# The second expert stage on token rows sorted by expert, instead of every expert on every token

## The reference

```
logits = xt @ router_w.T                      # 2048 tokens, 8 experts
topk_vals, topk_idx = top_k(logits, 2)
g = sigmoid(topk_vals); g = g / (g.sum(-1) + 1e-10)
for e in range(8):
    ge = sum(where(topk_idx == e, g, 0))      # 0 where e is not among the token's two
    h = silu(xt @ w_gate[e]) * (xt @ w_up[e]) # 128 -> 256
    out += ge * (h @ w_down[e])               # 256 -> 128
```

## Time and profile before

| | |
|---|---|
| median of three runs | 820.43 us |
| the profiled execution | 818.59 us |
| its span, first to last instruction | 816.6 us |
| granted clock of PE, mean | 0.996 |
| PE busy | 778.5 us, 95% |
| DVE busy | 627.8 us, 77% |
| ACT busy | 525.5 us, 64% |
| POOL busy | 420.0 us, 51% |

### The profile page before, as it was taken

The page is one execution under the profiler, slowest core; times in us unless marked ns, Lnnn a source line. Parts: engine busy times, 40 slices in busy tenths (PEclk is TensorE's granted clock), DMA queues, the critical chain, the costliest instruction groups (busy, mean ns, idle before and its releaser), DMA issues.

```text
span 816.6 us, 13532 instructions
## 1 busy us (share of the span) xinstructions
PE 778.5 (95%) x4328; PEld 544.7 (67%) x4328; DVE 627.8 (77%) x1600; ACT 525.5 (64%) x1163; POOL 420.0 (51%) x443
## 2 busy tenths in 40 slices
PE   4988899999889999999999999999999999999998
PEld 2666688886556666675666666766656667778886
DVE  7988688789799757779767778667696957877787
ACT  6556566655677767666767757667567755556654
POOL 1053999984334333333433334334335435699973
PEclk9999999999999999999999999999999999999999
DMA  8012454481000000000000000000010061254201
GB/s 231 3 43 27 107 128 97 67 302 77 1 2 1 1 1 2 1 2 1 2 1 1 2 1 1 1 2 0 2 40 14 27 91 44 54 113 92 77 13 53
DMA packets 51157, 35.16 MB, mean 43 GB/s; under 512 B 2656, under 2 KB 48608, under 8 KB 51088
## 3 DMA queue, kind: packets, MB, share of 16 engines
q1 hardware_dynamic: 51088, 34.30, 17.3%
HBM read 33.04 MB, written 1.25 MB: 42 GB/s over the span
## 4 chain that ended last, share of the span: by engine, by line
PE 77%; DVE 11%; ACT 4%; issue 4%; DMA 2%; POOL 2%; SPq 0%; DVEq 0%; POOLq 0%; ACTq 0%
PE psum L1004 14%; PE psum L986 12%; PE psum L971 11%; PE psum L249 10%; PE psum L524 8%; PE psum L250 8%; PE psum L251 8%; PE psum L928 4%; DVE prob L1104 2%; POOL hid_lo L816 2%; ACT x_norm L315 1%; DMA gate_all<-gates 1%; DVE hid L678 1%; DVE hid L658 1%; DVE ln_stats L264 1%
## 5 line engine op out<-in xcount | busy, mean ns | idle before, releaser
L1369 POOL TENSOR_SCALAR prob<-prob,ones 128x512 f32<-128x512 f32 x256 | 173.9, 692 | 272.2 <-DVE ones L1093 272.2
L1272 ACT ACTIVATE prob<-prob,ones 128x512 f32<-128x512 f32 x256 | 183.6, 719 | 124.4 <-DVE ones L1104 124.4
L816 POOL TENSOR_TENSOR hid_lo<-hid,hid_hi 128x512 fp32r<-128x512 f32 x125 | 187.1, 1512 | 73.6 <-ACT hid_hi L598 72.1
L1104 DVE CUSTOM_DVE_ANT_0 prob<-psum,bias_band 128x512 f32<-128x512 f32 x256 | 161.6, 687 | 71.3 <-PE psum L971 70.5
L678 DVE TENSOR_TENSOR hid<-hid,gate_all 128x512 f32<-128x512 f32 x118 | 117.6, 999 | 14.8 <-DMA gate_all<-gates 3.7
L1004 PE MATMUL psum<-probT,v 128*64 128x512 f32 x512 | 124.0, 605 | 0.0
L986 PE MATMUL psum<-ident,prob 128*128 128x128 f32 x1024 | 123.3, 273 | 0.0
L986 PEld LDWEIGHTS psum<-ident,prob 128*128 128x128 f32 x1024 | 114.6, 140 | 10.3 <-issue 2.8
L658 DVE TENSOR_TENSOR hid<-silu,psum 128x512 f32<-128x512 f32 x128 | 87.2, 683 | 43.6 <-PE psum L251 33.9
L591 ACT ACTIVATE silu<-psum 128x512 f32<-128x512 f32 x128 | 76.2, 597 | 65.4 <-PE psum L251 64.8
L598 ACT CAST hid_hi<-hid 128x512 fp32r<-128x512 f32 x128 | 78.5, 618 | 55.7 <-DVE hid L678 52.1
(11 more groups left out here) (165 smaller groups left out, 1204.3 us busy)
## 6 DMA issues: line engine op xcount, KB each, us to landing
gate_all<-gates SPq DMA_DIRECT2D x59, 256.0 KB, 5.4
bias_band<-bias_rows SPq DMA_DIRECT2D x16, 448.0 KB, 9.2
w_raw<-in_w_gate SPq DMA_DIRECT2D x16, 128.0 KB, 2.8
w_raw<-in_w_up SPq DMA_DIRECT2D x16, 128.0 KB, 2.8
w_raw<-in_w_down SPq DMA_DIRECT2D x16, 128.0 KB, 3.5
x_res<-in_x SPq DMA_DIRECT2D x4, 256.0 KB, 6.0
out<-x_res SPq DMA_DIRECT2D x3, 256.0 KB, 2.3
wqT<-in_WqT SPq DMA_DIRECT2D x1, 512.0 KB, 7.6
```

Source lines behind the costliest of these rows:

```text
L816: nc.gpsimd.tensor_tensor(m["hid_lo"][:, s % 2, half, :], m["hid"][:, s % DEEP, half, :], m["hid_hi"][:, s % 2, half, :].bitcast(F32), ALU ...
L1104: nc.vector.tensor_tensor_reduce(out=prob[:, buf, h, :], in0=bank[scores_home(n) + h][:, :], in1=row_bias, scale=-1.0, scalar=NEG_START, o ...
L1272: nc.scalar.activation(prob[:, buf, h, :], prob[:, buf, h, :], ACT.Exp, bias=peak[:, buf, h:h + 1], scale=-1.0, accum_out=total[:, buf, h: ...
L1369: nc.gpsimd.tensor_scalar(prob[:, buf, h, :], prob[:, buf, h, :], inv[:, buf, h:h + 1], 1.0, ALU.mult, ALU.mult).then_inc(a_n, 1)
```

## The change

The second expert stage no longer goes over all tokens for each expert. The tokens fall in three groups (chunks 0 and 1, chunk 2, chunk 3). For each group DVE finds the two experts of each token, and counts, with PE's help (`group_count`: a running sum over tiles on DVE, one over partitions by a matmul with a triangle of ones), for each choice its position among its expert's rows. Each expert gets whole blocks of 128 slots. That gives a slot number for each choice of each token, and an expert number for each block. POOL scatters the normalized rows of `x_norm` to their slots in memory (`xs`), one DMA by index for each tile and choice, 32 in all; SP loads them back with the slots on partitions. The numbers of blocks are fixed at their largest values, 23, 15 and 15; slots that nobody takes hold zeros, which SP writes beforehand.

A block on PE: a transpose of its rows (four blocks at a time, `sorted_turn`; ACT and DVE make the high and low halves), the expert's number read from memory into a register, three matmuls with the rows as the stationary side and the 512 gate and up columns of that expert moving, at the address that the register gives (`block_gate_up`), silu on ACT, product on DVE, two transposes (`block_turn`), a copy on ACT, and two full f32 matmuls with `w_down` of that expert (`block_down`). The results of four blocks leave PSUM at a time and are stored to memory (`ys`). POOL gathers them by slot number, 32 DMAs by index, and DVE adds each tile, times its gate, to `x` (`combine`, 32 operations). All eight experts' weights are held and split during the last attention slots (8 casts of 512 columns on ACT, 8 subtractions on POOL, in place of 6 and 6 of 256 columns). The gate broadcasts, the gates in PSUM, the split of the hidden product and the sums over experts in PSUM are gone from this stage. In the fourth batch entry one value projection moves from slots 7, 14, 15 to 14, 15, 18.

The diff, cut; buffers, semaphores, the routing and the calls in the slots are left out.

```diff
-            expert_buffers(1, hid_hi=QK_AT, hid_lo=QK_AT + H * P, hid=IN_BAND(40), silu=WV_AT, y_sum=R(0),
-                           w_hi=[IN_BAND(6), IN_BAND(9), R(68)], w_lo=[IN_BAND(12), IN_BAND(15), R(71)],
-                           w_raw=IN_BAND(0), routing=IN_BAND(18), gate_all=IN_BAND(24)),
...
+        GROUPS = [(0, 2 * QT), (2 * QT, 3 * QT), (3 * QT, 4 * QT)]
+        N_BLOCKS = [(2 * (n1 - n0) * P - E) // P + E for n0, n1 in GROUPS]
+        FIRST_BLOCK = [sum(N_BLOCKS[:g]) for g in range(len(GROUPS))]
+        ALL_BLOCKS = sum(N_BLOCKS)
...
+        QUADS = [(g, b, min(4, nb - b)) for g, nb in enumerate(N_BLOCKS) for b in range(0, nb, 4)]
+        BLOCK = [(q, j) for q, (g, b, n) in enumerate(QUADS) for j in range(n)]
...
+        def group_start(dve, g, home):
+            n, m = tiles_of(g), GRP[g]
+            dve.wait_ge(GS["pm"], g + 1)
+            counts = bank[home][:, 0:E * (n + 1)].rearrange("p (e n) -> p e n", e=E)
+            group_link(dve, nc.vector.tensor_scalar(m["nb"].unsqueeze(2), counts[:, :, n:n + 1], 1.0 / P,
+                                                    (P - 1) / (2.0 * P), ALU.mult, ALU.add))
+            group_link(dve, nc.vector.tensor_scalar(m["nb"], m["nb"], MAGIC, -MAGIC, ALU.add, ALU.add))
+            group_link(dve, nc.vector.tensor_tensor_scan(m["ce"], iota8[:, 1:2].to_broadcast([P, E]), m["nb"], 0.0,
+                                                         ALU.mult, ALU.add))
+            group_link(dve, nc.vector.tensor_tensor(m["st"], m["ce"], m["nb"], ALU.subtract))
+            nc.vector.scalar_tensor_tensor(out=by_expert(g, "pos"), in0=m["st"].unsqueeze(2).to_broadcast([P, E, n]),
+                                           scalar=float(P), in1=counts[:, :, 0:n], op0=ALU.mult,
+                                           op1=ALU.add).then_inc(GS["pb"], 1)
...
+        def group_blocks(dve, g):
...
+            group_link(dve, nc.vector.tensor_tensor(cmp, shared["count"][:, 0:nb].unsqueeze(2).to_broadcast([P, nb, E]),
+                                                    m["ce"].unsqueeze(1).to_broadcast([P, nb, E]), ALU.is_ge))
+            group_link(dve, nc.vector.tensor_reduce(m["bidf"], cmp, mybir.AxisListType.X, ALU.add))
+            nc.vector.tensor_scalar(m["bid"].bitcast(I32), m["bidf"], float(E - 1), None, ALU.min).then_inc(GS["bd"], 1)
...
+        def scatter_rows(pool, g, n, r):
+            pool.wait_ge(GS["sl"], g + 1)
+            pool.wait_ge(GS["zf"], 16 * len(GROUPS))
+            tile = GROUPS[g][0] + n
+            pool.wait_ge(LN[3]["xn"], tile // QT + 1)
+            at = r * tiles_of(g) + n
+            nc.gpsimd.indirect_dma_start(xs_dram[g][:, :], bass.IndirectOffsetOnAxis(
+                GRP[g]["slot"].bitcast(U32)[:, at:at + 1], 0), xn[:, tile, :], None).then_inc(GS["sc"][g], 16)
...
+        def gather_rows(pool, g, n, r):
+            pool.wait_ge(GS["yd"][g], 16 * sum(quad[0] == g for quad in QUADS))
+            tile, at = GROUPS[g][0] + n, r * tiles_of(g) + n
+            landed = GS["gd"][tile // QT] if g < 2 else GS["gt"][n]
+            nc.gpsimd.indirect_dma_start(ys_in[g][:, r, n, :], None, ys_dram[g][:, :], bass.IndirectOffsetOnAxis(
+                GRP[g]["slot"].bitcast(U32)[:, at:at + 1], 0)).then_inc(landed, 16)
...
+        def block_gate_up(pe, i):
+            q, j = BLOCK[i]
+            g, b, n = QUADS[q]
+            pe.wait_ge(GS["xl"], q + 1)
+            if i == FIRST_BLOCK[g]:
+                pe.wait_ge(GS["bd"], g + 1)
+            if i == 0:
+                pe.wait_ge(GS["ws"], E)
+            if i >= 3:
+                pe.wait_ge(GS["mul"], i - 2)
+            expert = pe.value_load(GRP[g]["bid"].bitcast(I32)[0:1, b + j:b + j + 1], min_val=0, max_val=E - 1)
+            expert_of[i] = expert
+            w = bass.ds(expert * (2 * FH), 2 * FH)
+            rows = slice(j * P, (j + 1) * P)
+            three(pe, bank[GATE_BANK + i % 3][:, :], xs_hi[:, q % 2, rows], xs_lo[:, q % 2, rows], ws_hi[:, w],
+                  ws_lo[:, w]).then_inc(GS["gu"], 1)
...
+        def block_turn(pe, i):
+            pe.wait_ge(GS["mul"], i + 1)
+            if i >= 2:
+                pe.wait_ge(GS["hc"], i - 1)
+            for h in range(MT):
+                last = nc.tensor.transpose(bank[HT_BANK + i % 2][:, h * P:(h + 1) * P],
+                                           s_hid[:, i % 3, h * P:(h + 1) * P], ident[:, :])
+            last.then_inc(GS["ht"], 1)
...
+        def block_down(pe, i):
+            q, j = BLOCK[i]
+            pe.wait_ge(GS["hc"], i + 1)
+            if i == 0:
+                pe.wait_ge(GS["wd"], 32)
+            if j == 0 and q > 0:
+                pe.wait_ge(GS["yc"], q)
+            for h in range(MT):
+                last = nc.tensor.matmul(bank[Y_BANK][:, j * P:(j + 1) * P], hT[:, i % 3, h * P:(h + 1) * P],
+                                        ws_down[:, bass.ds(expert_of[i] * (MT * D) + h * D, D)], start=(h == 0),
+                                        stop=(h == MT - 1))
+            last.then_inc(GS["dn"], 1)
...
+        def block_product(dve, i):
+            dve.wait_ge(GS["sg"], i + 1)
+            if i >= 3:
+                dve.wait_ge(GS["ht"], i - 2)
+            nc.vector.tensor_tensor(s_hid[:, i % 3, :], s_silu[:, i % 3, :], bank[GATE_BANK + i % 3][:, FH:2 * FH],
+                                    ALU.mult).then_inc(GS["mul"], 1)
...
+        def quad_out(dve, q):
+            g, b, n = QUADS[q]
+            dve.wait_ge(GS["dn"], QUAD_END[q])
+            nc.vector.tensor_copy(ys_out[g][:, b:b + n, :].rearrange("p b d -> p (b d)"),
+                                  bank[Y_BANK][:, 0:n * P]).then_inc(GS["yc"], 1)
...
+        def combine(dve, g, r, n):
+            tile = GROUPS[g][0] + n
+            c_done[0] += 1
+            gate = by_tile(g, "gw", 2)[:, n, r:r + 1]
+            nc.vector.scalar_tensor_tensor(out=x[:, tile, :], in0=ys_in[g][:, r, n, :], scalar=gate, in1=x[:, tile, :],
+                                           op0=ALU.mult, op1=ALU.add).then_inc(GS["cb"], 1)
...
+                sorted_turn(pe, 0)
                 transposes(SLOTS - 1)
                 pv(SLOTS - PV_LAG + 1)
                 pe.wait_ge(a_m, 2 * SLOTS)
-                part(0, 1)
+                block_gate_up(pe, 0)
                 for n in range(SLOTS - QT, SLOTS):
                     pv(n)
-                part(1, 0)
-                part(1, 1)
-                pe.wait_ge(a_x, part_count(B - 1, 0))
+                block_gate_up(pe, 1)
+                pe.wait_ge(a_ea, SLOTS)
+                pe.wait_ge(a_eb, SLOTS)
+                block_turn(pe, 0)
+                block_gate_up(pe, 2)
+                pe.wait_ge(GS["pb"], 2)
                 for half in range(2):
                     project_out(B - 1, 1, half)
-                part(2, 0)
-                pe.wait_ge(a_ea, SLOTS)
-                down(pe, 1, 0)
-                part(2, 1)
-                part(3, 0)
-                pe.wait_ge(a_eb, SLOTS)
-                down(pe, 1, 1)
-                part(3, 1)
-                part(4, 0)
+                block_turn(pe, 1)
+                sorted_turn(pe, 1)
                 pe.wait_ge(a_o, B * PAIRS)
-                down(pe, 1, 2)
-                part(4, 1)
...
+                block_down(pe, 0)
+                for i in range(3, ALL_BLOCKS):
+                    q, j = BLOCK[i]
+                    block_gate_up(pe, i)
+                    block_turn(pe, i - 1)
+                    block_down(pe, i - 2)
+                    if j == 1 and q + 1 < len(QUADS):
+                        sorted_turn(pe, q + 1)
+                    if i == 7:
+                        ln_turn(pe, 3, 3, JOB_BANK)
+                    if i == 10:
+                        group_logits(pe, 2, JOB_BANK)
+                    if i == 16:
+                        pe.wait_ge(GS["rs"], 3)
+                        group_count(pe, 2, JOB_BANK)
+                block_turn(pe, ALL_BLOCKS - 1)
+                block_down(pe, ALL_BLOCKS - 2)
+                block_down(pe, ALL_BLOCKS - 1)
...
+                sorted_low(dve, 0)
+                for i in range(ALL_BLOCKS):
+                    q, j = BLOCK[i]
+                    block_product(dve, i)
+                    last_chunk(i)
+                    combined(i)
+                    if j == 2 and q + 1 < len(QUADS):
+                        sorted_low(dve, q + 1)
+                    if i >= 2 and BLOCK[i - 2][1] == QUADS[BLOCK[i - 2][0]][2] - 1:
+                        quad_out(dve, BLOCK[i - 2][0])
+                quad_out(dve, len(QUADS) - 1)
+                dve.wait_ge(GS["gd"][2], 16 * 2 * QT)
+                dve.wait_ge(GS["gw"], 3)
+                for r in range(2):
+                    if r == 1:
+                        dve.wait_ge(GS["cb"], c_done[0])
+                    for n in range(QT):
+                        combine(dve, 1, r, n)
+                for n in range(QT):
+                    dve.wait_ge(GS["gt"][n], 32)
```

(32 more changed lines are left out.)

568 lines of the change are left out of this document (353 added, 215 removed).

## The result

| | time, us (median) | span of the profiled run | mean granted clock |
|---|---|---|---|
| before | 818.79 | 816.6 | 0.996 |
| after | 827.95 | 827.7 | 0.958 |

The changed kernel takes 1.0115 times as long, interval 1.0084 to 1.0147: slower by 9 us, where 15 us less were forecast.

The account below looks back on a forecast made before the run. PE, busy 95% of the span, was taken as the bound. The terms 660 + 6 + 10.7 + 102.3 + 5 + 1.5 + 17.6 gave a span of 803 us, and 2 us over the span gave 805; range 783 to 850.

Parts of the forecast that it names:

- In the block stage: Second expert stage: 5 us of PE waiting for DVE's norm and routing, 1.5 filling and draining, later groups' scatters at nothing.
- Pace: Time per block on PE: 1.93 us, from 1.63 for the stream plus 0.3 for DVE's order; 53 blocks 102.3 us.
- 10.7 + 102.3 + 5 + 1.5: Block stage in us: attention work left on PE, 53 blocks, PE waiting for DVE's norm and routing, filling and draining.
- The loaded address: Register load before each block's gate/up matmuls on PE: taken as 0.7 us, between bounds of 0.08 and 1.4.
- Attention: Last quarter of attention: new routing, scatters and POOL's larger subtractions cost 6 us, from 2 to 14; first block about 666.
- The new end: After the last down product: copy, store, eight gathers 1.3 us apart, additions, store; 17.6 us in place of 4.65.
- Rival 1: Register load before each block costs next to nothing: pace 1.65 us, 15 us less, 790 us; chance 0.20.
- Rival 2: Register load before gate/up lies open: 2.55 us a block, 53 blocks 135 us, measured time of 838 us; chance 0.20.
- Rival 3: Index DMAs slow on POOL, 2.5 us each: end 27 us, normalizations pushed, 10 + 8 us more, 823; chance 0.09.
- Rival 4: PE's clock stays at the lower level in the block stage: array work 3.0 us a block, 862 us; chance 0.05.
- Rival 5: Rows come late in the block stage, group 2's scatters queued behind group 1's: 5 to 10 us; no chance given.

Follow-up runs that it names:

- e4: Changed kernel with scatters of group 2 and gathers of groups 0 and 1 each waiting for a block's product, so copies by index are spaced; 798.16 us.
- e10: e4 with the scatters of groups 1 and 2 left in a row as in the changed kernel, only the gathers spaced; 805.18 us.
- e1: Changed kernel with plain copies issued by POOL (wrong rows) in place of the scatters of groups 1 and 2 and all gathers; 791.45 us.
- e2: Changed kernel with plain copies issued by SP (wrong rows) in place of the scatters of groups 1 and 2 and all gathers; 789.24 us.
- e8: e4 with the copies by index let go two at a time every second block; 796.91 us.
- e3: Changed kernel without the register load: each block's expert is fixed in the program at a constant address, copies still in a row; 783.39 us.
- e7: e4 with the register load of the next block moved right behind the gate/up matmuls of the block before; 792.44 us.
- e16: Changed kernel with only the register load moved behind gate/up of the block before, copies by index still in a row; 791.1 us.
- e11: Changed kernel with the upper 64 of 128 partitions left out of the scatters of groups 1 and 2, all gathers and their additions; 829.93 us.

## Why the prediction was wrong, point by point

- **The failed step** is in "In the block stage": "The scatters of the later groups go out from about block 18, ... at nothing", and with it that the gathers of groups 0 and 1 had no price at all. I charged copies by index as work on POOL, and did not ask what they do to others. Measured: 29.8 us (after against e4), more than the whole forecast gain of 15. The eight scatters of group 2 in a row are 7.0 of it (e10 against e4), the gathers of groups 0 and 1 in a row the other 22.8 (after against e10).
- **Pace.** Forecast 1.93 us; where nothing disturbs it 1.71 to 1.78 (e1, e2, e4, e8). The stage was to take 119.5 us (10.7 + 102.3 + 5 + 1.5), of which some 2.4 (the work that the new order puts ahead) come before the first gate/up. From there to the end of the last matmul it takes 108.2 us in e4 (669.1 to 777.3), and 140.2 in the changed kernel. So these terms were too dear by about 9 us, and without the hold-up the forecast of 805 would have been 7 us too high.
- **The loaded address.** I took 0.7 us, from bounds of 0.08 and 1.4; the trace has 0.30, with 0.17 of register work behind it. It does lie open where the change put it: the fixed expert has a pace of 1.37 against 1.71, and 798.16 - 783.39 = 14.8 us are 0.28 a block (e3 has its copies in a row, e4 spaced; in both no silu is late). Moved behind gate/up some of it is hidden (e4 to e7: 5.7 us). The median load of 302 ns is nearer the 200 ns of the Trainium skill ("Runtime: NRT & Kernel Launch", Instruction fetch mechanics) than my 0.7; the measured value stands.
- **Attention.** Forecast 6 us more, the first block at about 666. Measured: the first gate/up stands at 669.3, where it stood at 659.95 before, and some 2.4 us of work (8 transposes of attention, 4 products with v, the first transposes of rows) have moved ahead of it; that leaves about 7. The size was near, the place was not: the transposes before it are only 1.6 us late (659.54 against 657.92), and most of the rest is PE standing 1.9 us for a copy of DVE in the middle of the last transposes and 2.9 us just ahead of the first gate/up.
- **The new end.** Forecast 17.6 us with gathers 1.3 apart; measured 18.1 (809.6 to 827.7), gathers 1.25 apart. Right, and from bounds a factor of 4.5 apart.
- **Rival 1**, the free load at 790 with a pace of 1.65, is about what e16 reaches (791.1 at 1.66), though its load is not free but stands elsewhere. **Rival 2**, the open load, had the right sign for a wrong reason: its place is right, its price is 0.28 and not 1.05 a block. **Rival 3** saw the copies by index as the danger, but as slow on POOL: they take 943 to 976 ns each beside DVE's products as in the empty end, so the rule of the Trainium skill on the port pair ("SBUF — State Buffer", on the DVE blocks DMA trap) does not show here. It speaks of DVE in a mode that takes two ports, as a copy within SBUF can; DVE's products here read PSUM, so this case does not test it. The harm is on PE's signals. **Rival 4**: the clock did fall, to a mean of 0.69, but behind the idle time; with the same instructions and no late signals it is 1.00 (e16). **Rival 5** did not happen: in e4 the rows of group 2 have landed at 737.7, and its first gate/up starts at 749.5.
- The range of 783 to 850 held the time, by luck: its upper end came from rival 2, which did not happen. Faster at 0.61 was on the wrong side.

## What to carry to other kernels

Where a stream of copies by index runs beside a dense chain of small steps on PE, ACT and DVE, space the copies to the pace of the steps (a wait on a count that is there anyway) rather than let POOL issue all it can: such waits were worth 30 us of 828 here. Put a register load behind matmuls that keep the array busy, not ahead of the matmuls that use it. And when three engines are idle together and the releaser is "remote", compare the end of the producer with the start of the consumer: the step between them is what is slow.

## What the runs showed of the hardware that was not expected

- While copies by index were issued every 1.25 us, PE's signals came up to 11.0 us after the end of a gate/up and 12.9 us after that of a down product (14.8 us after a gate/up in e11); four or five held signals then arrived within 0.2 us. ACT's signals were not held: in blocks 16 to 52 of the changed kernel each product starts at most 0.2 us after its silu. DVE's were not held where the trace shows PE waiting for one (0.05 us at 755.11).
- A copy of 128 rows by index takes POOL 0.95 us, 1.25 from one to the next, for gathers as for scatters; beside DVE's work it is no slower.
- A register load on PE takes 0.30 us. 53 of them with their register work cost 14.8 us when placed ahead of the matmuls that need them (e4 against e3).
- Two kernels that differ in the place of one 0.3 us instruction are 37 us apart (e16 and after). With the copies spaced the same move is worth 5.7 (e4 and e7), so most of it is that e16 escapes the hold-up.
